# Head of a transformer tower: later splits of the third to fifth weight tiles and another order of the first tokens' steps

## The reference, cut to what matters

```python
h = _L0_tok_ref(x, L0_tok_kernel, L0_tok_bias, L0_tok_pos_emb)   # 8 shards, clipped index, + 8 * bias + pos
h = h + _L0_attn_ref(_layernorm(h, axis=-1), L0_attn_w_qkv, L0_attn_w_dense)   # 8 groups of 4 heads, head width 128
h = h + _L0_ffn_ref(_layernorm(h, axis=-1), L0_ffn_up, L0_ffn_down, L0_ffn_perm)
```

## Time and profile before

| | before |
|---|---|
| median of 3 runs | 2604.17 us (2603.53 to 2606.53) |
| the profiled execution, whole | 2604.64 us |
| its span | 2602.7 us |
| TensorE busy | 2584.7 us (99%) |
| VectorE busy | 1194.3 us (46%) |
| ScalarE busy | 989.3 us (38%) |
| GpSimd busy | 318.4 us (12%) |

### The profile page before, as it was taken

The page is one execution under the profiler, slowest core; times in us unless marked ns, Lnnn a source line. Parts: engine busy times, 40 slices in busy tenths (PEclk is TensorE's granted clock), DMA queues, the critical chain, the costliest instruction groups (busy, mean ns, idle before and its releaser), DMA issues.

```text
span 2602.7 us, 35197 instructions
## 1 busy us (share of the span) xinstructions
PE 2584.7 (99%) x12982; PEld 2111.9 (81%) x12982; DVE 1194.3 (46%) x3147; ACT 989.3 (38%) x2612; POOL 318.4 (12%) x266
## 2 busy tenths in 40 slices
PE   8999999999999999999999999999999999999998
PEld 6888888888878877888887887788888778878884
DVE  5444444554444434455444443445445344434444
ACT  5544444454343333224333334322433333332232
POOL 5233334333000000100000000010000000000002
PEclk9999999999999999999999999999999999999999
DMA  5556668655544444644443443463444444434432
GB/s 168 182 196 223 212 218 276 219 202 205 181 135 161 146 140 133 211 146 139 146 158 133 161 144 137 146 209 137 146 150 146 143 142 161 146 133 144 142 128 97
DMA packets 135190, 425.67 MB, mean 164 GB/s; under 512 B 15918, under 2 KB 15918, under 8 KB 135022
## 3 DMA queue, kind: packets, MB, share of 16 engines
q1 hardware_dynamic: 127488, 398.00, 44.2%
q0 software_dynamic: 7424, 25.17, 3.4%
q10 hardware_dynamic: 110, 0.26, 0.0%
HBM read 322.71 MB, written 100.66 MB: 163 GB/s over the span
## 4 chain that ended last, share of the span: by engine, by line
PE 97%; DMA 1%; ACT 0%; DVE 0%; POOL 0%; issue 0%; ACTq 0%; POOLq 0%; SPq 0%; DVEq 0%
PE fb L556 22%; PE fb L558 22%; PE fb L557 22%; PE tp L591 6%; PE pv L556 3%; PE sc L556 3%; PE sc L557 3%; PE sc L558 3%; PE pv L558 3%; PE pv L557 3%; PE sc L643 2%; PE fb L652 2%; PE sc L582 1%; PE pv L605 1%; PE pv L637 1%; PE fb L637 1%
## 5 line engine op out<-in xcount | busy, mean ns | idle before, releaser
L556 PE MATMUL fb<-xn_hi,w_both 128*128 128x512 f32 x1504 | 596.0, 396 | 0.0
L558 PE MATMUL fb<-xn_hi,w_both 128*128 128x512 f32 x1504 | 587.5, 391 | 0.0
L557 PE MATMUL fb<-xn_lo,w_both 128*128 128x512 f32 x1504 | 586.2, 390 | 0.0
L556 PE MATMUL fb<-at_hi,w_both 128*128 128x512 f32 x992 | 394.0, 397 | 0.0
L558 PE MATMUL fb<-at_hi,w_both 128*128 128x512 f32 x992 | 387.7, 391 | 0.0
L557 PE MATMUL fb<-at_lo,w_both 128*128 128x512 f32 x992 | 386.3, 389 | 0.0
L829 ACT ACTIVATE prob<-sc,neg_max 128x128 f32<-128x128 f32 (+3 forms) x512 | 263.0, 526 | 286.4 <-DVE neg_max L960 286.4
L556 PEld LDWEIGHTS fb<-xn_hi,w_both 128*128 128x128 f32 x1504 | 282.4, 188 | 75.4 <-issue 18.8
L1015 DVE TENSOR_TENSOR hacc<-hacc,fb 128x512 f32<-128x512 f32 x256 | 175.8, 687 | 349.3 <-PE fb L558 348.9
L558 PEld LDWEIGHTS fb<-xn_hi,w_both 128*128 128x128 f32 x1504 | 282.3, 188 | 60.3
L557 PEld LDWEIGHTS fb<-xn_lo,w_both 128*128 128x128 f32 x1504 | 282.7, 188 | 57.2
(11 more groups left out here) (211 smaller groups left out, 3466.6 us busy)
## 6 DMA issues: line engine op xcount, KB each, us to landing
w_both<-qkv_halves SPq DMA_DIRECT2D x268, 512.0 KB, 3.6
w_both<-dense_halves SPq DMA_DIRECT2D x192, 512.0 KB, 3.8
qkv_halves<-w_both SPq DMA_DIRECT2D x96, 512.0 KB, 3.8
dense_halves<-w_both SPq DMA_DIRECT2D x64, 512.0 KB, 3.4
w_raw<-in_w_qkv SPq DMA_DIRECT2D x116, 256.0 KB, 4.1
w_raw<-in_w_dense SPq DMA_DIRECT2D x64, 256.0 KB, 3.8
h_rows<-hacc SPq DMA_DIRECT2D x32, 256.0 KB, 2.3
h_tok<-in_pos SPq DMA_DIRECT2D x12, 512.0 KB, 7.3
```

The costliest lines, as they stand in the source:

```text
L556: pe.matmul(dst, a_hi, b_hi, start=first, stop=False)
L557: pe.matmul(dst, a_hi, b_lo, start=False, stop=False)
L558: return pe.matmul(dst, a_lo, b_hi, start=False, stop=last)
```

## The change

The string `START` and the table `FIRST_SPLITS` change; nothing else does.

```diff
-START = ("A G0 G1 G2 G3 w0 w1 w2 J0 J1 B0 B1 La0 B2 Lb0 B3 La1 J2 X0 X1 w3 Lb1 C0 B4 B5 La2 J3 X2 X3 Lb2 C1 w4 B6 B7 La3 "
+START = ("A G0 G1 G2 G3 w0 w1 w2 J0 B0 J1 B1 La0 B2 Lb0 B3 La1 X0 X1 w3 Lb1 J2 B4 B5 La2 X2 X3 C0 Lb2 C1 J3 w4 B6 B7 La3 "
          "X4 X5 Lb3 a0 C2 a1 X6 X7 C3 a2 a3 Q0 K Q1 V")
...
 FIRST_SPLITS = [Step(k, 0, 0, i) for k, i in (
-    ("B", 1), ("Lb", 0), ("X", 1), ("Lb", 1), ("X", 3), ("X", 4), ("X", 5), ("Lb", 3), ("X", 7), ("C", 3), ("Q", 0))]
+    ("B", 1), ("Lb", 0), ("Lb", 1), ("X", 3), ("C", 1), ("X", 4), ("X", 5), ("Lb", 3), ("X", 7), ("C", 3), ("Q", 0))]
```

## The result

| | before | after |
|---|---|---|
| median time, 20 runs each | 2603.85 us (2603.12 to 2606.53) | 2609.05 us (2607.95 to 2612.09) |
| ratio | | 1.0020, 95% interval 1.0013 to 1.0026 |
| profiled execution, whole / span | 2604.64 / 2602.7 us | 2612.09 / 2609.4 us |
| median span | 2601.7 us (33 runs) | 2606.9 us (20 runs) |
| `a0` starts (profile) | 28.46 us | 35.58 us |

The change costs 5.2 us. The forecast said +2.1, with a range up to 2609.0: the direction was right, the size less than half, and the range missed by 0.05 us. The execution profiled first was the slowest of the twenty, 2.5 us above the median span. A second profile, further down, has a span of 2608.1, longer than 19 of the twenty. So the lines of both show what can happen; what is usual has to be inferred from the spans.

The account below looks back on a forecast made before the run. TensorE hardly pauses from `a0` on, so only that start counts: it moves from 28.46 to 30.57, +2.1 us, giving 2606.7 on the profiled execution and 2606.3 against the median; 8-in-10 range 2603.8 to 2609.0.

Parts of the forecast that it names:

- Step 4: `C0` and the third split behind `X2 X3`: `w4` at 26.65 instead of 24.20, `a0` at 30.57, +2.1 us.
- Steps 1 to 3: `B0` before `J1` and `Lb1` before a weight split gain 2.6 us on ScalarE; `J2` behind `X0 X1` leaves 0.07.
- step 1: `B0` ahead of `J1` on VectorE: its statistic hides in idle time, tile 0's sums end 0.60 us earlier.
- The clock rival: TensorE's 2.9 us pause ahead of `w4` drops its clock; `a0` up to 2.9 later, +5.0, 2609.2; chance 0.12.
- The recorded sign of being wrong: A product behind `w4` at half pace, listed among the signs that would show the forecast wrong.
- The starting point: `a0`, the first projection on TensorE, starts at 28.46 us before the change; the shift was counted from there.
- the faster one: ScalarE's freed wait reaches `a0`: 2603.4, or 2602.7 with the whole 1.44 us passed on; chance 0.10.
- The smaller loss: `J2` holds `B4` less, root near 23.0, only `C0`'s place costs: +0.6, 2604.8; chance 0.12.
- Steps 5 and 6: Later weight splits cost nothing, loads landing 4 us or more ahead; the fourth tile's `X6` keeps 1.8 us of slack.

Follow-up runs that it names:

- j2_j3_s4_later: Kernel before with `J2` and `J3` behind the turned tokens of the tile ahead and the fifth split behind `C1`: 2609.09 us, ratio 1.0019.
- after_w6_w5: Changed kernel plus two matmuls that nobody reads, one ahead of `B4` and one ahead of `w4`: 2608.28 us, ratio 1.0016 against the kernel before.
- after_w5: Changed kernel plus one matmul that nobody reads, ahead of `w4`: 2608.52 us, ratio 1.0016 against the kernel before.
- after_w6_w5_s3_later: Changed kernel plus two unread matmuls, ahead of `B4` and `w4`, and the fourth split behind `C1` too: 2607.58 us, ratio 1.0012 against the kernel before.
- c0_behind: Kernel before with only `C0` moved behind `X2 X3`: 2607.49 us, ratio 1.0010.
- j2_j3_behind: Kernel before with only `J2` and `J3` moved behind the turned tokens of the tile ahead: 2611.61 us, ratio 1.0028.
- after_c0_back: Changed kernel with `C0` back ahead of `B4`: 2610.07 us, ratio 1.0023 against the kernel before.
- after_j_back: Changed kernel with additions `J1`, `J2`, `J3` back at their old places: 2607.14 us, ratio 1.0010 against the kernel before.
- splits_and_j1: Kernel before with only the later splits and `J1` behind `B0`: 2603.44 us, ratio 0.9997.

## Why the prediction was wrong in size

Spans: 2606.9 less 2601.7 is 5.2. The forecast's sum was 2.1. Step 4 of it failed: it let `w4`, `B6` and `B7` "keep their 2.28 us", which took 3.80 and, in the second profile, 4.24 (26.41 to 30.65), and it had `J3` "hidden by 0.2". Term by term:

- **Steps 1 to 3 were right in the second profile.** Aligned by the second addition, `B4`, the root and `w4` stand where the working put them, to 0.02 us. The 1.35 us on `B4` for `J2` behind `X0 X1` was right, and so was that ScalarE's gain ends at the third root. In the first profile step 1 wasn't: the first addition came at 11.14, `B0` ran at half pace, and its statistic (14.24) put the second addition at 14.85, where POOL stretched it to 2.48 us. The forecast allowed 0.65 us there, and it was 2.2; `B4` comes 3.7 us later than in the second profile.
- **Step 4, the size of `J3`.** "Hidden by 0.2" took 1.2 us for the fourth addition. Behind `X3`'s subtraction it falls on the low part of the split that stands behind `X3`, and takes 2.2. It is hidden no more and costs 0.76. This was argued from an addition's duration without asking what runs on POOL beside it; `j2_j3_s4_later` shows the hold.
- **The clock rival, given 0.12, came in both profiles of the changed kernel.** The recorded sign of being wrong, a product behind `w4` at half pace, is in both. Its mechanism and place were right (the pause ahead of `w4`; 2.9 forecast, 2.76 measured), its price of 2.9 the upper bound (2.84 in the second profile). For the other runs it is inferred: with `J3` held and the level kept, `a0` would come at 31.08 and the span at 2605.2; the two shortest of the twenty are 2605.3, and the median is 1.6 above them. In the median the level costs 1.0 (by `after_w6_w5`) to 1.4 (by the sum below). It should have been a term of the sum. That pauses of 1.1 us left the pace alone says nothing about one of 2.8. The rules of the Trainium skill, TensorE: Matmul & The Clock Gate, on what the clock means for kernels, spoke for this rival. The granted clock of 0.50 behind the pause agrees in kind, but that section names longer gaps than this one; here the level fell even behind 1.99 us and once held behind 2.76, so the measurement decides.
- **The starting point.** The forecast moved `a0` from 28.46, but the usual run has it at 27.6: 0.9. In the changed kernel the third split stands behind `Lb1`, and neither of its profiles waits for that tile, so the late landing lengthened the start of the sum and not its end. The whole time of that run (2604.64) looked ordinary since 1.94 lay around its span, where 2.7 is usual.

2.1, 0.9 and 0.76 make 3.8; the rest, 1.4, is put down to the level. With the level held (`after_w6_w5`) 4.2 of the 5.2 are left, 0.4 more than the 3.8; 0.2 of it may be a later start, as in its profile, the rest I can't place. So the terms are shown in the profiled runs, and their split in the median is an estimate.

- **The rivals.** The condition of the faster one, a root before 22.0, is not met (24.18 and 27.89). The smaller loss didn't come. Steps 5 and 6 were right: behind `a0` TensorE waits for no weight, and the longest wait of both profiles after is 0.7 us for `xn_lo`.
- **The slack left.** The sum's 2606.3 would have been 2608 with `J3` and the start; the range ended at 2609.0 for one mishap at a time, and three came together. That the median missed it by only 0.05 us is luck: the range ended near the clock rival's 2609.2, and the 5.0 of that rival was made up otherwise. The forecast also took 0.2% for the least that a measurement of this kernel can tell; the ratio's interval, 1.0013 to 1.0026, is clear of 1.

## What to carry to other kernels

Before an instruction is moved, lay the timeline of the other engine that it can take turns with beside the new place: the fourth addition cost nothing where it was moved to, until POOL's split over it was counted. When a change opens a pause in TensorE, count the products behind it at half pace unless rows of this kernel show a pause that long survived. And where a single transfer's landing sets the baseline, take a second profile, or compare the span with the median span, before shifting numbers from it.

## What the runs showed of the hardware

- TensorE's level fell in the profiles behind pauses of 1.99 us (`after_w5`, one matmul late, and `after_w6_w5_s3_later`), 2.15 (`B0` of the changed kernel's first profile), 2.76 (both profiles of the changed kernel, in the second only from `B6` on, and `c0_behind`) and 3.60 (`j2_j3_behind`, `after_c0_back`). It held behind 1.99 (`after_w6_w5`), 2.63 (`j2_j3_s4_later`) and 2.76 (`after_j_back`), and in seven profiles behind a pause of 1.79 to 1.88. What decides between 1.99 and 2.76 us stays open.
- VectorE's addition of 128x1024 with both inputs in the on-chip memory takes 1.22 us alone and up to 2.48 beside POOL's subtraction of 1.27. It works the other way too: in `splits_and_j1` a low part of POOL that met such an addition took 2.01 us instead of 1.27.
- The first gather's addition started between 8.70 and 11.14 us in 17 profiles of nearly the same head. How much of the scatter between runs comes from that start isn't shown: the three profiles of before have it at 9.59, 9.52 and 9.30, with spans of 2602.7, 2601.5 and 2601.7.
